# Two small loads of a three-stage matrix kernel move to earlier places in the load queue

## The reference

```python
base = jnp.einsum('bsi,oi->bso', x, W)              # layer 0
low = jnp.einsum('bsi,bir->bsr', x, lora_A[labeler_index])
y = x + base + jnp.einsum('bsr,or->bso', low, lora_B_w) * 0.5
...
base_out = jnp.einsum('bti,oi->bto', y, W1) + b     # layer 1
lora_h = jnp.einsum('bti,bir->btr', y, lora_As[adapter_mapping])
z = y + base_out + jnp.einsum('btr,bro->bto', lora_h, lora_Bs[adapter_mapping]) * 2.0
```

## Time and profile before

| | |
|---|---|
| median of three runs | 295.98 us (293.93 to 296.96) |
| the profiled execution's own time | 294.4 us |
| its span, first to last instruction | 292.7 us |
| TensorE matmul (PE) | 286.7 us busy, 98% of the span |
| VectorE (DVE) | 223.2 us, 76% |
| ScalarE (ACT) | 143.5 us, 49% |
| DMA | 29.21 MB, mean 100 GB/s |
| chain that ended last | PE 93%, SPq 3%, DMA 2%, issue 1% |

### The profile page before, as it was taken

The page is one execution under the profiler, slowest core; times in us unless marked ns, Lnnn a source line. Parts: engine busy times, 40 slices in busy tenths (PEclk is TensorE's granted clock), DMA queues, the critical chain, the costliest instruction groups (busy, mean ns, idle before and its releaser), DMA issues.

```text
span 292.7 us, 3668 instructions
## 1 busy us (share of the span) xinstructions
PE 286.7 (98%) x1340; PEld 239.6 (82%) x1340; DVE 223.2 (76%) x265; ACT 143.5 (49%) x194; POOL 5.0 (2%) x13
## 2 busy tenths in 40 slices
PE   8979999999999999999999999999999999999996
PEld 5858888888888888888888888888988888888885
DVE  5557998898988989999985999839295956687400
ACT  5377539452563862827282632637474463505021
POOL 0000300000000000010000000000010000000000
PEclk9999999999999999999999999999999999999999
DMA  7389800220645101116432438240101100012222
GB/s 252 93 301 394 271 2 2 72 73 0 202 114 152 36 2 36 36 24 172 168 113 68 140 106 290 91 129 37 38 0 72 72 2 0 0 72 91 91 99 81
DMA packets 18628, 29.21 MB, mean 100 GB/s; under 512 B 2994, under 2 KB 5426, under 8 KB 18610
## 3 DMA queue, kind: packets, MB, share of 16 engines
q1 hardware_dynamic: 18610, 28.98, 30.2%
HBM read 20.58 MB, written 8.39 MB: 99 GB/s over the span
## 4 chain that ended last, share of the span: by engine, by line
PE 93%; SPq 3%; DMA 2%; issue 1%; ACT 0%; DVE 0%
PE ps L917 93%; SPq L196 2%; SPq L194 1%; DMA label_t<-in_labels 1%; DMA b0raw<-in_b 1%; ACT b0s L447 0%; DVE b0s L449 0%; DVE keep_s L731 0%
## 5 line engine op out<-in xcount | busy, mean ns | idle before, releaser
L917 PE MATMUL ps<-brh,ar0h 128*128 128x512 f32 (+1 forms) x180 | 69.2, 390 | 0.1
L917 PE MATMUL ps<-brl,ar0h 128*128 128x512 f32 (+1 forms) x180 | 68.3, 385 | 0.0
L917 PE MATMUL ps<-brh,ar0l 128*128 128x512 f32 (+1 forms) x180 | 68.2, 384 | 0.0
L233 ACT ACTIVATE brh<-w_B 128x1024 fp32r<-128x1024 f32 (+1 forms) x40 | 38.8, 969 | 57.6 <-PE ps L917 50.6
L917 PE MATMUL ps<-brh,ar1h 128*128 128x512 f32 x160 | 62.5, 391 | 0.0
L917 PE MATMUL ps<-brl,ar1h 128*128 128x512 f32 x160 | 62.3, 390 | 0.0
L917 PE MATMUL ps<-brh,ar1l 128*128 128x512 f32 x160 | 62.3, 389 | 0.0
L234 DVE TENSOR_TENSOR brl<-w_B,brh 128x1024 fp32r<-128x1024 f32 (+1 forms) x40 | 44.5, 1113 | 18.5 <-ACT brh L233 18.3
L917 PEld LDWEIGHTS ps<-brh,ar0h 128*128 128x128 f32 x180 | 34.3, 191 | 7.4 <-ACT ar0h L233 0.8
L917 PEld LDWEIGHTS ps<-brh,ar0l 128*128 128x128 f32 x180 | 33.8, 188 | 6.8
L917 PEld LDWEIGHTS ps<-brl,ar0h 128*128 128x128 f32 x180 | 33.9, 188 | 6.5
(11 more groups left out here) (116 smaller groups left out, 355.7 us busy)
## 6 DMA issues: line engine op xcount, KB each, us to landing
w_B<-in_x SPq DMA_DIRECT2D x32, 256.0 KB, 2.8
out_z<-keep_s SPq DMA_DIRECT2D x23, 256.0 KB, 2.0
w_B<-in_w SPq DMA_DIRECT2D x16, 256.0 KB, 5.1
w_A<-in_w SPq DMA_DIRECT2D x16, 256.0 KB, 4.9
raw<-in_b SPq DMA_DIRECT2D x64, 32.0 KB, 1.7
out_z<-keep_w SPq DMA_DIRECT2D x8, 256.0 KB, 2.1
raw<-in_a SPq DMA_DIRECT2D x8, 128.0 KB, 2.2
a1raw<-in_a SPq DMA_DIRECT2D x8, 64.0 KB, 1.8
```

What stands on the lines that cost most here:

```text
L233: act(waits + spare, lambda e: e.activation(hi, src, ACT.Copy, scale=scale), h, 0.2 + 0.43 * wide)
L917: ins = eng.matmul(out_ap, lhs, rhs, start=first, stop=False, skip_group_check=True)
```

## The change

Two due times written by hand: the label load's falls from 7.0 to 4.0, and the load of `b0raw` gets one, 9.0, where it had only the derived one. No instruction is added or removed.

```diff
         transfer([], lambda: [(label_t[:, :], labels)], s_lab, tk("labels"), 1)
-        plan.jobs[-1].due = 7.0
+        plan.jobs[-1].due = 4.0
...
         transfer([], lambda: [(b0raw[:, :, :].rearrange("p k r -> p (k r)"), b0[:, :])], s_b0, tk("b0"), 128)
+        plan.jobs[-1].due = 9.0
```

## The result

The changed kernel takes 292.63 us, the median of 11 runs (292.40 to 293.33), against 295.77 us for 11 runs of the kernel before (293.93 to 296.96). The ratio is 0.9909, with a 95% interval of 0.9884 to 0.9935. The profiled execution took 292.63 us, its span is 290.9 instead of 292.7. So two profiles differ by 1.8 us, and the medians by 3.1; the difference between these two numbers is what most of the experiments are about.

A forecast was written before the change was run, and what follows sets the result against it. TensorE, busy 286.7 of 292.7 us, bounds the kernel; time is gained only where it stops. Closing the `b0s` stop (1.84 plus 0.14 restart, other costs nothing) gives 295.3 - 1.98 = 293.3 us, range 291.9 to 295.3.

The forecast's parts named there:

- The stop closes and the end moves with it: TensorE's wait for `b0s` between first product and `down`: earlier `b0raw` removes it, and the unbroken matmuls behind begin earlier.
- Its size, 1.98 us: At `across` on TensorE: start at 18.68 instead of 20.66 us, from 1.84 us lost plus 0.14 of slow restart.
- The sum: Whole kernel: gain 1.98 us, bounds 1.36 and 1.98; span from 292.7 to 290.7, time 295.3 - 1.98 = 293.3 us.
- The cover: Quarter 3 splits of the first product: pushed back 2.0 us at most, within 3.2 us of slack, so costed at nothing.
- the slower rival: ScalarE's list ahead of quarter 3: the copy waits for a late `b0raw` and blocks later splits; 295.9 us, chance 0.04.
- The supplies behind: Operands of `across`, narrow matmuls, second and third products: on time though asked 1.98 us earlier; narrowest slack 1.36, third product.
- the estimate of 7.3 for `b0raw`: Load queue: issued around 4.0 us, `b0raw` lands at 7.3, 2.5 quarters behind the label's 5.56, in order of bytes.
- its slack of 6 us: `b0s` ahead of `down`: complete near 10.6 us and wanted at 16.87, so 6 us to spare.
- The level: Starting time of the whole kernel: 295.3 us, the mean of all four known times, from which the gain is taken.
- the range's low end: Whole kernel's time: 291.9 us, the fastest known run, 293.93, less the 1.98 gain.
- more than the stop: Behind the stop on TensorE: unprofiled runs have slow matmuls there, 2.9 us more gain, 290.4 us; chance 0.04.

## Why the prediction held, step by step

**The stop closes and the end moves with it: right.** No matmul waits for `b0s`, and every place behind it moved by the same 1.77 us. The rows of the chain and of the waits carried this.

**Its size, 1.98 us: 0.2 too much in the profile.** All of the difference lies ahead of the stop's place. The last matmul of the first product starts at 16.85 and not 16.64: its first started 0.07 later, and the late quarter 1 and the pace of the first matmuls took the rest. The sum held the first product fixed, and its start is not fixed: over the profiles here its last matmul starts between 15.9 and 16.9, because the first four take 1.0 us in some and 1.7 to 1.9 in others (5.14 to 6.86 before). The slow ones start 0.43 apart, the spacing of the lower clock level in the second profile of the kernel before, and the spacing falls to 0.23 at a time that differs from profile to profile: the start varies with the moment at which the clock rises. As long as TensorE then stops for `b0s`, this is hidden by the stop; once the stop is closed, it shows, and when the start is quick the second product's quarter 3 takes part of it back.

**The cover: right.** The splits of quarter 3 ended at 13.34 where 14.81 was the need, 1.47 us of slack where I had left 1.2 at worst. The copy started at 10.25 and not at 9.07, as the split of quarter 2 was itself later. Nothing blocked ScalarE, and the slower rival did not come.

**The supplies behind: right for the profile, and thinner than I read them.** The slack of the second product was 1.91 before and is 1.28 now, that of the third is unchanged. But what `across` and the second product use hangs on the label, and I took its landing as one number, 5.56, in the order of the bytes. In the second profile of the kernel before it landed at 2.68 + 3.14 = 5.82, while VectorE waited for A11's quarter 1, issued ahead of it, until 6.46:

```profile
2.68 3.14 DMA label_t<-in_labels
```

```profile
6.46 0.29 DVE L439 TENSOR_TENSOR w_A<-w_A,eye 128x128 f32<-128x128 f32 x1 [0.47 <-DMA w_A<-in_w]
```

So loads need not land in the order of their issue, and the estimate of 7.3 for `b0raw` had no firm ground; its slack of 6 us did not rest on it, as ScalarE took the copy up only at 10.25, without a wait. Behind four quarters the label's landing varied: in seven profiles the loads of `a1raw` began between 10.12 and 11.66. Behind two, with `b0raw` ahead of the reads, they began at 10.13, 10.14 and 10.18, since SyncE's own issues end last there. This is what the label's part of the change is for, and the sum gave it 0.2 us.

**The level: the step that was mis-sized.** I took 1.98 from a mean of 295.3 that held runs of lost clock, and gave the slow matmuls behind the stop a chance of 0.04, on the word of one profile that did not have them. The start's rows priced them at 2.9 us; they cost 1.7 in windows, and fall on 40 of 94 runs. The mean of before, 295.20, is the 294.24 of its full-clock runs and 1.0 for the others. The change takes both: 1.7 for the stop (294.24 to 292.56) and 1.0 for the clock (295.20 to 294.24) are the 2.6 between the means, 295.20 and 292.56. That is why 292.63 came out and not 293.3. It is still inside the range because the range's low end was set from the fastest run; the sum did not hold the second part, and the rival "more than the stop", which did, had the right kind of cause and a price too high. The rule of the Trainium skill ("TensorE: Matmul & The Clock Gate", section "What's actually happening"), that an idle stretch can bring the throttled clock back, I had set against one row. Over many runs the clock agrees with the rule: it fell in 40 of 94 runs with the stop, in eight of ten with the longer one, and in none of ten with the stop filled.

## What to carry to other kernels

A stop of the busiest engine can cost more than its length: look at the granted clock of many runs, not at one profile, before a stop is priced. A load that waits for addresses should have its index load issued early enough that the issuing engine, not the landing, ends last; otherwise, as in this kernel, the landing's scatter can show up far behind it. And when the work behind a stop becomes the new chain, what was hidden beside the stop, here the pace of the start and the second product's supply, comes into the time.

## What the hardware did that I had not expected

In the kernel before, whose two profiles show stops of 1.68 and 1.96 us of idle time, the granted clock fell in 40 of 94 runs and not in the others. It fell 1.3 us after work had resumed in the profile with 1.96, and during the standstill in the one with 4.78; what decides in a single run, these runs do not settle. With only the label moved, where the profile shows 1.47 us of idle time, it fell in none of ten. A 64-byte load issued at the same 2.68 us behind the same four loads of 256 KB landed after 2.88 us in one profile and after 4.19 in another. The matmuls of the program's first microseconds start 0.43 apart although the view of windows prints a granted clock of 1.00 there. The record of the clock has no entry before 4.3 to 7.3 us, and a stretch without an entry is printed as 1.00; in all thirteen traces the spacing falls from 0.43 to 0.23 where the first entry begins (6.66 in the first profile of the kernel before), so the start is best read from the spacing.
